# Another order for the first three memory tiles of a fused attention and expert kernel, with matmuls ahead of the first input

## The chip, the cores and the metric

The kernel runs on one core of a Trainium2 chip. A core has five engines, each with its own instruction stream: TensorE (PE, its weight loads PEld), VectorE (DVE), ScalarE (ACT), GpSimd (POOL) and SyncE (SP), which only starts transfers. The engines meet through semaphores. The metric is the device time of one execution in microseconds (us), as a median of runs.

## What is computed

One layer with a memory attention and a mixture of experts over 4 batches of 1024 tokens, 128 features each. The change touches only the attention part, cut here to what matters:

```python
z = x @ W_in                                   # 128 + 32 + query columns
z_mem = conv(pad(z[..., :160]), conv_k)        # 4 taps along the tokens
k_val = z_mem[..., :128]                       # 32 heads x 4
s_raw = z_mem[..., -32:]
log_p = clip(score_scale * s_raw, -20, 20)
p_w = exp(log_p + log_tw)                      # decayed scores; log_tw from softplus(slopes) * distance
phi = k_val[..., None] * theta                 # 8 angles each: 1024 phases per token
num_re, num_im = cumsum(p_w * cos(phi)), cumsum(p_w * sin(phi))
den = cumsum(p_w)
y = silu(read-out of (num / den) with the queries)
x = layernorm(x + y @ W_out)                   # then router, top 2 of 8 experts, shared expert, layernorm
```

## The kernel before

Four stages follow each other in each engine's stream: `memory` (the attention), `dispatch` (router, shared expert, writing the tokens to tables), `routed` (the experts) and `finish`. The change lies in `memory`.

The 4096 tokens are 32 memory tiles of 128 tokens: tile `i` is block `j = i // 4` of batch `b = i % 4`. A tile passes through these steps, which I call by the names of the helper functions:

- `phases(i)` on TensorE (L540): keys `k_val` times the angles `th_f` into the 1024 columns of PSUM tile `ph`. It waits for `frac_done` of the tile before, since `ph` exists once.
- `rounding(i)` on ScalarE (L356): the phases in turns, plus a large constant, so that they are rounded to whole turns in `feat`.
- `fraction(i)` on VectorE (L678): the phase's fraction of a turn.
- `sine(i)` (L360 absolute value, L361 Sin) and `cosine(i)` (L365) on ScalarE.
- `weigh(i)` on GpSimd (two instructions, L451): both halves of `feat` times the weights `p_tok`. It waits for `feat_done` (set by `cosine`) and for `p_kept`.
- `sums(i)` on TensorE (L556): the cumulative sum over the tile's tokens, into `nsum`.
- `read_out(i)` (two instructions, L690) and `reduce(i)` (L699) on VectorE: the sums times the queries, added up. `last_row(i, h)` on ScalarE (L374) copies the last row for the next tile of the batch; GpSimd's `carry` adds it in by a transfer.

The keys of a block of four tiles come from `value(j, t)`, four matmuls of 512 columns (L496), one per tap, into `pk`; `k_part(j)` copies them to `k_val` (L350). The weights `p_tok` are made in three chunks of 256, 256 and 512 tokens (`CHUNKS`), 32 heads x 4 batches on the partitions: `scores(n)` (L486) makes the raw scores, `keep_z(n)` copies them (L334), `logits(n)` is seven dependent instructions on VectorE (L641, three of L643, L645, L646, L649) that end in `lp_ready`, `exp_p(n)` is the exponential on ScalarE (L339), `turn_p(n)` the transposition (L507) and `keep_p(n)` the copy to `p_tok` (L344). Chunk 0 serves tiles 0 to 7, chunk 1 tiles 8 to 15, chunk 2 the rest.

What `logits` needs once is made before it on VectorE: the convolution's weights `wconv` (L622), the small operations on `sp` for the softplus of the slopes (L615 to L635, a dependent chain on one column), and the inputs of GpSimd's first instruction, which makes `th_f` (L425).

The order is written by hand: each engine has a list of calls ahead of its loop over the 32 tiles, and the loop runs ahead by `rounding(i + 3)`, `fraction(i + 3)`, `phases(i + 3)` and by `sine(i + 2)`, `cosine(i + 2)`. ScalarE's loop body of tile 0 also holds `exp_p(1)` and `exp_p(2)` with two loads of function tables around them, between `last_row(0, 1)` and `rounding(4)`. Each engine works its list in order, so a wait holds all that is behind it.

## Time and profile before

| what | value |
|---|---|
| median of 3 runs (lowest to highest) | 535.51 us (534.37 to 537.81) |
| the profiled execution's own time | 533.17 us |
| its span, first to last instruction | 531.3 us |
| busy: PE, DVE, ACT, POOL | 440.9, 376.9, 355.7, 310.1 us |
| instructions | 7487 |

The span is what the trace covers; a little under 2 us of the execution's time lie around it. The attention ends about 235 us in, dispatch about 330, the experts about 495. In the table of the 40 slices, each 13.3 us long, VectorE's digits over the attention are

```profile
DVE  7497999998999999999756566282333334554296
```

so from the fifth slice, at 53 us, to the end of the attention VectorE is busy for nine tenths or more nearly throughout, and in the four slices before that it is not.

### The profile page before, as it was taken

The page shows a single profiled execution, that of the slowest core. Times are in us where ns is not written, and L with a number is a line of the kernel's source. Part 1 is how long each engine was busy: PE and PEld are TensorE (multiplying, and loading weights), DVE is VectorE, ACT ScalarE, POOL GpSimd, SP SyncE. Part 2 cuts the span into 40 slices and gives each one's busy share as a digit, 9 for nine tenths or more (in the row PEclk, how much of TensorE's full clock was granted, in tenths as well). Part 3 has the DMA queues.
Part 4 walks back from the last instruction along what each step waited for, and adds up shares of the span by engine and source line. Part 5 has one row for each costly group of instructions (what it writes and reads, how often), then busy time and mean ns, then how long its engine had stood idle before and what let it go on. Part 6 is the DMA issues. An engine that isn't in the chain of part 4 may idle for free.

```text
span 531.3 us, 7487 instructions
## 1 busy us (share of the span) xinstructions
PE 440.9 (83%) x2153; PEld 288.9 (54%) x2153; DVE 376.9 (71%) x839; ACT 355.7 (67%) x534; POOL 310.1 (58%) x261
## 2 busy tenths in 40 slices
PE   5758899998999988856879999959999999999100
PEld 1213344433343433323657877749999999999100
DVE  7497999998999999999756566282333334554296
ACT  1848799998999999922355655617666676666244
POOL 3251567777677777761277877732555554655440
PEclk9987999999999999979689999979999999999655
DMA  7010010109866654000011111122222221221463
GB/s 258 0 40 0 2 41 1 43 15 388 313 234 226 226 209 162 1 1 1 6 48 50 47 46 51 52 70 66 67 80 68 74 63 54 68 61 46 148 227 99
DMA packets 39448, 48.55 MB, mean 91 GB/s; under 512 B 5408, under 2 KB 25058, under 8 KB 38896
## 3 DMA queue, kind: packets, MB, share of 16 engines
q1 hardware_dynamic: 34048, 39.06, 21.7%
q0 software_dynamic: 5216, 8.70, 5.3%
q10 hardware_dynamic: 144, 0.31, 0.2%
q8 instruction: 18, 0.29, 0.2%
q14 instruction: 22, 0.18, 0.1%
HBM read 19.17 MB, written 29.11 MB: 91 GB/s over the span
## 4 chain that ended last, share of the span: by engine, by line
PE 36%; DVE 33%; issue 12%; POOL 9%; ACT 7%; DMA 3%; SPq 0%; ACTq 0%; DVEq 0%; POOLq 0%
PE routed_ph L1312 12%; PE routed_po L1325 12%; DVE memory_prod L690 10%; DVE memory_y_raw L699 9%; POOL table_scratch L1017 5%; DVE memory_feat L678 4%; PE dispatch_sph L877 3%; PE dispatch_spo L887 3%; POOL memory_feat L451 2%; PE routed_px L1300 2%; DVE memory_query L673 1%; PE memory_nsum L556 1%; ACT memory_feat L356 1%; DVE finish_xo L1528 1%; ACT memory_feat L360 1%
## 5 line engine op out<-in xcount | busy, mean ns | idle before, releaser
L451 POOL TENSOR_TENSOR memory_feat<-memory_feat,memory_p_tok 128x1024 f32<-128x1024 f32 x64 | 121.6, 1923 | 57.8 <-ACT memory_feat L365 57.7
L556 PE MATMUL memory_nsum<-memory_feat,tri 128*128 128x512 f32 x256 | 118.7, 607 | 15.1 <-DVE memory_prod L690 7.3
L1288 POOL DMA_INDIRECT pick_scratch<-routed_ob,routed_xg x71 | 71.5, 1007 | 73.0 <-DVE routed_ob L1409 57.8
L556 PEld LDWEIGHTS memory_nsum<-memory_feat,tri 128*128 128x128 f32 x256 | 48.1, 194 | 76.5 <-issue 72.5
L690 DVE TENSOR_TENSOR memory_prod<-memory_nsum,memory_query 128x1024 f32<-128x1024 f32 x64 | 75.4, 1217 | 2.8 <-PE memory_nsum L556 2.7
L1017 POOL DMA_INDIRECT table_scratch<-dispatch_xrow,dispatch_slot x64 | 63.1, 986 | 18.9 <-issue 18.0
L699 DVE TENSOR_REDUCE memory_y_raw<-memory_prod 128x128 f32<-128x2048 f32 x32 | 73.1, 2285 | 1.0
L1358 ACT ACTIVATE routed_rel<-routed_ph 128x512 f32<-128x512 f32 x71 | 42.3, 597 | 45.9 <-PE routed_ph L1312 45.9
L1312 PE MATMUL routed_ph<-routed_xs,routed_w1c 128*128 128x256 f32 (+1 forms) x368 | 72.3, 340 | 0.0
L1409 DVE TENSOR_SCALAR routed_ob<-routed_po,routed_xg 128x128 f32<-128x128 f32 x71 | 22.6, 348 | 69.7 <-PE routed_po L1325 69.7
L1325 PE MATMUL routed_po<-routed_w2c,routed_hid 128*128 128x128 f32 x568 | 71.1, 275 | 0.5 <-ACT routed_hid L1367 0.5
L1325 PEld LDWEIGHTS routed_po<-routed_w2c,routed_hid 128*128 128x128 f32 x568 | 67.0, 192 | 0.8 <-ACT routed_hid L1367 0.7
L374 ACT COPY memory_last_rows<-memory_nsum 32x1024 f32<-32x1024 f32 x56 | 55.1, 1005 | 16.3 <-DVE memory_prod L690 14.0
L1312 PEld LDWEIGHTS routed_ph<-routed_xs,routed_w1c 128*128 128x128 f32 x368 | 57.3, 193 | 4.8
L540 PE MATMUL memory_ph<-setup_th_f,setup_k_val 64*128 64x512 f32 x128 | 38.0, 671 | 13.3 <-DVE memory_feat L678 12.5
L678 DVE SCALAR_TENSOR_TENSOR memory_feat<-memory_feat,memory_ph 128x1024 f32<-128x1024 f32 x32 | 38.5, 1203 | 11.5 <-ACT memory_feat L356 11.5
L1367 ACT ACTIVATE routed_hid<-routed_rel 128x512 f32<-128x512 f32 x71 | 42.5, 638 | 0.0
L496 PE MATMUL memory_pk<-memory_xT,memory_wconv 128*128 128x512 f32 x64 | 37.7, 690 | 0.4 <-issue 0.4
L887 PEld LDWEIGHTS dispatch_spo<-w,dispatch_shid 128*128 128x128 f32 x256 | 32.1, 192 | 9.8 <-issue 8.8
L365 ACT ACTIVATE memory_feat<-memory_feat,memory_half_pi 128x1024 f32<-128x1024 f32 x32 | 36.4, 1139 | 0.0
L887 PE MATMUL dispatch_spo<-w,dispatch_shid 128*128 128x128 f32 x256 | 34.3, 279 | 1.0 <-DVE y_all L1123 0.9
L877 PE MATMUL dispatch_sph<-dispatch_x1T,w 128*128 128x512 f32 x64 | 35.0, 633 | 0.0
(177 smaller groups left out, 623.8 us busy)
## 6 DMA issues: line engine op xcount, KB each, us to landing
table_scratch<-memory_blank SPq DMA_DIRECT2D x68, 260.0 KB, 2.9
finish_pick<-pick_scratch SPq DMA_DIRECT2D x16, 256.0 KB, 5.4
routed_xg<-table_scratch SPq DMA_DIRECT2D x25, 130.0 KB, 2.2
x_tok<-x SPq DMA_DIRECT2D x4, 512.0 KB, 3.8
w<-w_up SPq DMA_DIRECT2D x2, 1024.0 KB, 9.1
w<-w_down SPq DMA_DIRECT2D x2, 1024.0 KB, 11.1
out<-finish_xo SPq DMA_DIRECT2D x8, 256.0 KB, 2.3
routed_xg<-table_scratch SPq DMA_DIRECT2D x21, 65.0 KB, 1.9
```

Of the source, the lines that this page charges most:

```text
L374: nc.scalar.copy(last_rows[32 * b:32 * b + 32, h * NF:(h + 1) * NF], nsum[96:P, h * NF:(h + 1) * NF]).then_inc(rows_kept, 1)
L451: last = nc.gpsimd.tensor_tensor(v, v, pv, ALU.mult)
L556: last = nc.tensor.matmul(nsum[:, o:o + 512], tri[:], feat[:, i % U, h, q * 512:(q + 1) * 512], start=True, stop=True)
L678: nc.vector.scalar_tensor_tensor(v, v, -ROUND, ph[:], ALU.add, ALU.subtract).then_inc(frac_done, 1)
L690: nc.vector.tensor_tensor(prod[:, h, :].rearrange("p (q r c) -> p q r c", q=KQ, r=REP), nv, qv.unsqueeze(2).broadcast_to([P, KQ, REP, HM]) ...
L699: nc.vector.tensor_reduce(y_raw[:, j % 2, b, :], prod[:].rearrange("p h (c m) -> p c h m", m=M), AX.XY, ALU.add).then_inc(red_done, 1)
L877: nc.tensor.matmul(sph[q % 2][:], w1[:, E, q * P:(q + 1) * P], x1T[:, g % XR].rearrange("p t c -> p (t c)"), start=True, stop=True).then_i ...
L887: last = nc.tensor.matmul(spo[:, t * D:(t + 1) * D], shid[:, g % 2, q, t * P:(t + 1) * P], w2[:, E, q, :], start=(q == 0), stop=(q == FC - 1))
L1017: nc.gpsimd.indirect_dma_start(out=table, in_=xrow[:, r, n, :], in_offset=None, out_offset=bass.IndirectOffsetOnAxis(ap=slot[:, r, n:n + 1 ...
L1288: nc.gpsimd.indirect_dma_start(out=pick_dram, in_=ob[:, u, h, :], in_offset=None, out_offset=bass.IndirectOffsetOnAxis(ap=xg[:, t % XU, h, ...
L1312: last = nc.tensor.matmul(ph[s][:, q * n:(q + 1) * n], w1c[:, u, q * P:(q + 1) * P], xs[:, s, 0:n], start=True, stop=True)
L1325: last = nc.tensor.matmul(po[:, h * D:(h + 1) * D], hid[:, s, q * n + h * P:q * n + (h + 1) * P], w2c[:, u, q, :], start=(q == 0), stop=(q ...
```

## The change

Nothing after the loop over the tiles is changed. The lists ahead of the loops are, and some places in PSUM:

- TensorE first runs five matmuls of 256 columns on a tile of ones (`WARMING`), whose result is overwritten. VectorE sets the ones first for that.
- The keys of block 0 are made in two steps: `value_first` only those of tile 0 (four matmuls of 128 columns into `pq`), `value_rest` those of tiles 1 to 3 (four of 384 columns into `pk`). `k_first` and `k_rest` copy them. So `k_kept` and `k_done` count one more everywhere.
- `phases(0)` comes right behind `scores(0)`; `rounding(0)` comes before `exp_p(0)` on ScalarE.
- `wconv` is made before the small operations on VectorE, and so before GpSimd's `th_f`.
- VectorE's list is logits 0, fraction 0, logits 1, fraction 1, logits 2, fraction 2, query 0. It was logits 0, fraction 0, logits 1, fraction 1, fraction 2, query 0, logits 2.
- `turn_p(0)` comes behind `phases(1)`, `sums(0)` before the loop and so ahead of `phases(3)`, `k_part(1)` behind `cosine(1)`.
- The raw scores lie in `nsum` instead of `ph`.

The core of the diff:

```diff
-        z_at = (ph[:, 0:256], nsum[:, 0:256], nsum[:, 512:1024])
-        p_at = (nsum[:, 1024:1280], pq_v[:, 0:256], pq_v)
+        z_at = (nsum[:, 0:256], nsum[:, 512:768], nsum[:, 1024:1536])
+        p_at = (nsum[:, 1536:1792], pq_v[:, 0:256], pq_v)
...
+            def k_first():
+                act.wait_ge(k_done, 1)
+                nc.scalar.copy(k_val[:, 0, 0:P], pq_v[:, 0:P]).then_inc(k_kept, 1)
+
+            def k_rest():
+                act.wait_ge(k_done, 2)
+                nc.scalar.copy(k_val[:, 0, P:], pk[:, P:]).then_inc(k_kept, 1)
...
+            k_first()
             keep_z(0)
-            k_part(0)
+            rounding(0)
+            k_rest()
+            keep_z(1)
             exp_p(0)
             nc.scalar.activation(warm[:], half_pi[:], ACT.Sin).then_inc(warmed, 1)
             act.wait_ge(warmed, 1)
-            rounding(0)
+            sine(0)
+            keep_z(2)
             keep_p(0)
-            keep_z(1)
-            keep_z(2)
-            sine(0)
+            cosine(0)
             rounding(1)
-            cosine(0)
-            k_part(1)
             sine(1)
             rounding(2)
             cosine(1)
+            k_part(1)
...
+            def value_first():
+                pe.wait_ge(halo_set, 1)
+                pe.wait_ge(wconv_made, 1)
+                pe.wait_ge(x_in[0], 16)
+                for t in range(TAPS):
+                    last = nc.tensor.matmul(pq_v[:, 0:P], wconv[:, t, :], xT[:, 0, t:t + P],
+                                            start=(t == 0), stop=(t == TAPS - 1))
+                last.then_inc(k_done, 1)
+
+            def value_rest():
+                for t in range(TAPS):
+                    last = nc.tensor.matmul(pk[:, P:], wconv[:, t, :], xT[:, 1:, t:t + P],
+                                            start=(t == 0), stop=(t == TAPS - 1))
+                last.then_inc(k_done, 1)
...
+            pe.wait_ge(ones_set, 1)
+            for n in range(WARMING):
+                nc.tensor.matmul(ph[:, 0:256], one_row[:, 0:P], one_row[:, 0:256], start=True, stop=True)
             pe.wait_ge(w_arrived, 16)
+            value_first()
             scores(0)
-            pe.wait_ge(halo_set, 1)
-            pe.wait_ge(wconv_made, 1)
-            for t in range(TAPS):
-                value(0, t)
-            pe.wait_ge(z_kept, 1)
             pe.wait_ge(th_made, 1)
             phases(0)
-            pe.wait_ge(tabs_in, 32)
-            turn_p(0)
+            value_rest()
             scores(1)
             scores(2)
             phases(1)
+            pe.wait_ge(tabs_in, 32)
+            turn_p(0)
             pe.wait_ge(wq_made, 1)
             queries(0)
             for t in range(TAPS):
@@ -578,6 +605,7 @@
             phases(2)
             pe.wait_ge(p_kept, 1)
             pe.wait_ge(z_kept, 3)
+            sums(0)
             for i in range(NT):
...
+            dve.wait_ge(w_arrived, 16)
+            nc.vector.tensor_tensor(wconv[:], taps_row, w_in[:, 0:KH].unsqueeze(1).broadcast_to([P, TAPS, KH]),
+                                    ALU.mult).then_inc(wconv_made, 1)
             link(nc.vector.tensor_scalar(sp[:, 2:3], slope, -1.0, None, ALU.mult))
...
             fraction(0)
             logits(1)
             fraction(1)
+            logits(2)
             fraction(2)
             q_part(0)
-            logits(2)
```

How the instructions stand on VectorE around the third chunk of scores (`setup_lp`; 512 columns) and the tiles' `memory_feat`, before:

```order
L649 SCALAR_TENSOR_TENSOR setup_lp<-setup_dist,memory_sp,setup_lp 128x256 [waits memory_dist_in1,memory_dchain]
L678 SCALAR_TENSOR_TENSOR memory_feat<-memory_feat,memory_ph 128x1024 [waits memory_rnd_done] x2
L673 COPY memory_query<-memory_pq 128x512 [waits memory_q_done]
L641 TENSOR_SCALAR setup_lp<-setup_zs,setup_consts 128x512 [waits memory_z_kept]
L643 SCALAR_TENSOR_TENSOR setup_lp<-setup_zs,setup_consts,setup_lp 128x512 [waits memory_dchain] x3
L645 TENSOR_SCALAR setup_lp<-setup_lp,setup_consts 128x512 [waits memory_dchain]
L646 TENSOR_SCALAR setup_lp<-setup_lp 128x512 [waits memory_dchain]
```

and after the change:

```order
L678 SCALAR_TENSOR_TENSOR setup_lp<-setup_dist,memory_sp,setup_lp 128x256 [waits memory_dist_in1,memory_dchain]
L707 SCALAR_TENSOR_TENSOR memory_feat<-memory_feat,memory_ph 128x1024 [waits memory_rnd_done]
L670 TENSOR_SCALAR setup_lp<-setup_zs,setup_consts 128x512 [waits memory_z_kept]
L672 SCALAR_TENSOR_TENSOR setup_lp<-setup_zs,setup_consts,setup_lp 128x512 [waits memory_dchain] x3
L674 TENSOR_SCALAR setup_lp<-setup_lp,setup_consts 128x512 [waits memory_dchain]
L675 TENSOR_SCALAR setup_lp<-setup_lp 128x512 [waits memory_dchain]
L678 SCALAR_TENSOR_TENSOR setup_lp<-setup_dist,memory_sp,setup_lp 128x512 [waits memory_dchain]
L707 SCALAR_TENSOR_TENSOR memory_feat<-memory_feat,memory_ph 128x1024 [waits memory_rnd_done]
L702 COPY memory_query<-memory_pq 128x512 [waits memory_q_done]
```

The five rows of the third chunk now stand ahead of the third tile's remainder and of the copy of the first queries; before they stood behind both.

On ScalarE, from the exponential of the first chunk (`setup_pT`) on, before:

```order
L339 ACTIVATE setup_pT<-setup_lp 128x256 [waits memory_lp_ready]
L382 ACT_TABLE_LOAD
L382 ACTIVATE memory_warm<-memory_half_pi 128x1
L356 ACTIVATE memory_feat<-memory_ph 128x1024 [waits memory_ph_done,memory_warmed]
L344 COPY memory_p_tok<-memory_nsum 128x256 [waits memory_p_turned]
L334 COPY setup_zs<-memory_nsum 128x256 [waits memory_z_done]
L334 COPY setup_zs<-memory_nsum 128x512 [waits memory_z_done]
L360 ACTIVATE memory_feat<-memory_feat 128x1024 [waits memory_frac_done]
L361 ACTIVATE memory_feat<-memory_feat 128x1024
L356 ACTIVATE memory_feat<-memory_ph 128x1024 [waits memory_ph_done]
L365 ACTIVATE memory_feat<-memory_feat,memory_half_pi 128x1024 [waits memory_abs_done]
```

and after the change:

```order
L341 ACTIVATE setup_pT<-setup_lp 128x256 [waits memory_lp_ready]
L395 ACT_TABLE_LOAD
L395 ACTIVATE memory_warm<-memory_half_pi 128x1
L370 ACTIVATE memory_feat<-memory_feat 128x1024 [waits memory_frac_done,memory_warmed]
L371 ACTIVATE memory_feat<-memory_feat 128x1024
L336 COPY setup_zs<-memory_nsum 128x512 [waits memory_z_done]
L346 COPY memory_p_tok<-memory_nsum 128x256 [waits memory_p_turned]
L375 ACTIVATE memory_feat<-memory_feat,memory_half_pi 128x1024 [waits memory_abs_done]
L366 ACTIVATE memory_feat<-memory_ph 128x1024 [waits memory_ph_done]
L370 ACTIVATE memory_feat<-memory_feat 128x1024 [waits memory_frac_done]
```

The first rounding (L356 before) has gone from behind the table load to ahead of these rows. The second (L366 after) has gone from ahead of the first cosine (L365 before, L375 after) to behind it.

## Rows read from the trace of the kernel before

**Rows 1.** The page, part 4: the chain that ended last, by engine.

```profile
PE 36%; DVE 33%; issue 12%; POOL 9%; ACT 7%; DMA 3%; SPq 0%; ACTq 0%; DVEq 0%; POOLq 0%
```

**Rows 2.** Stretches of the span: busy time (instructions), PEclk, DMA share, GB/s.

```profile
30.00:40.00 10.00, 5.65 (x12) 2.11 (x10) 9.79 (x8) 3.95 (x4) 6.17 (x4) 0.84 0.18 53
...
60.00:100.00 40.00, 38.52 (x109) 16.41 (x109) 39.83 (x33) 38.17 (x42) 27.78 (x19) 1.00 0.11 28
```

**Rows 3.** Timeline, VectorE, to 21 us. Columns: start us, us, engine, line, operation.

```profile
4.78 2.47 DVE L622 TENSOR_TENSOR memory_wconv<-setup_consts,setup_w_in 128x512 f32<-128x512 f32 x1
...
7.18 0.14 DVE L626 TENSOR_SCALAR memory_sp<-memory_sp 128x1 f32<-128x1 f32 x1
...
13.23 0.48 DVE L649 SCALAR_TENSOR_TENSOR setup_lp<-setup_dist,memory_sp,setup_lp 128x256 f32<-128x256 f32 x1
...
17.91 0.35 DVE L641 TENSOR_SCALAR setup_lp<-setup_zs,setup_consts 128x256 f32<-128x256 f32 x1
...
20.57 0.48 DVE L649 SCALAR_TENSOR_TENSOR setup_lp<-setup_dist,memory_sp,setup_lp 128x256 f32<-128x256 f32 x1
```

**Rows 4.** Timeline, VectorE, the third scores and the first sums.

```profile
27.14 1.22 DVE L678 SCALAR_TENSOR_TENSOR memory_feat<-memory_feat,memory_ph 128x1024 f32<-128x1024 f32 x1 [4.95 <-ACT memory_feat L356]
...
28.88 1.53 DVE L641 TENSOR_SCALAR setup_lp<-setup_zs,setup_consts 128x512 f32<-128x512 f32 x1
...
30.45 3.85 DVE L643 SCALAR_TENSOR_TENSOR setup_lp<-setup_zs,setup_consts,setup_lp 128x512 f32<-128x512 f32 x3
...
34.86 2.02 DVE L646 TENSOR_SCALAR setup_lp<-setup_lp 128x512 f32<-128x512 f32 x1
...
36.91 2.28 DVE L649 SCALAR_TENSOR_TENSOR setup_lp<-setup_dist,memory_sp,setup_lp 128x512 f32<-128x512 f32 x1
...
39.11 1.21 DVE L678 SCALAR_TENSOR_TENSOR memory_feat<-memory_feat,memory_ph 128x1024 f32<-128x1024 f32 x1
...
48.45 1.22 DVE L678 SCALAR_TENSOR_TENSOR memory_feat<-memory_feat,memory_ph 128x1024 f32<-128x1024 f32 x1 [3.55 <-ACT memory_feat L356]
```

**Rows 5.** The chain in order of time: start us, us, what.

```profile
32.76 0.76 DVE setup_lp L643
```

**Rows 6.** Timeline, GpSimd, to 39 us.

```profile
4.75 1.95 POOL L425 TENSOR_TENSOR setup_th_f<-setup_consts,setup_theta 128x1024 f32<-128x1024 f32 x1 [4.31 <-DVE setup_theta L617]
...
22.05 3.78 POOL L451 TENSOR_TENSOR memory_feat<-memory_feat,memory_p_tok 128x1024 f32<-128x1024 f32 x2 [12.01 <-ACT memory_feat L365]
...
28.22 3.96 POOL L451 TENSOR_TENSOR memory_feat<-memory_feat,memory_p_tok 128x1024 f32<-128x1024 f32 x2 [2.38 <-ACT memory_feat L365]
...
34.65 3.99 POOL L451 TENSOR_TENSOR memory_feat<-memory_feat,memory_p_tok 128x1024 f32<-128x1024 f32 x2 [2.47 <-ACT memory_feat L365]
```

**Rows 7.** Timeline, ScalarE, to 44 us.

```profile
13.75 0.42 ACT L339 ACTIVATE setup_pT<-setup_lp 128x256 f32<-128x256 f32 x1 [0.18 <-DVE setup_lp L649]
...
15.48 0.20 ACT L382 ACTIVATE memory_warm<-memory_half_pi 128x1 f32<-128x1 f32 x1
...
16.89 0.88 ACT L334 COPY setup_zs<-memory_nsum 128x256 f32<-128x256 f32 x2
...
18.03 1.06 ACT L360 ACTIVATE memory_feat<-memory_feat 128x1024 f32<-128x1024 f32 x1 [0.26 <-DVE memory_feat L678]
...
33.44 1.14 ACT L365 ACTIVATE memory_feat<-memory_feat,memory_half_pi 128x1024 f32<-128x1024 f32 x1
...
41.48 2.14 ACT L374 COPY memory_last_rows<-memory_nsum 32x1024 f32<-32x1024 f32 x2 [6.91 <-DVE memory_prod L690]
```

**Rows 8.** Timeline, TensorE, to 31 us.

```profile
5.84 1.08 PE L486 MATMUL memory_ph<-memory_xT,setup_w_in 128*32 128x256 f32 x8 [5.84 <-DMA memory_xT<-x_T]
...
13.71 1.13 PE L540 MATMUL memory_ph<-setup_th_f,setup_k_val 64*128 64x512 f32 x4 [0.77 <-ACT setup_k_val L350]
...
20.07 3.60 PE L496 MATMUL memory_pk<-memory_xT,memory_wconv 128*128 128x512 f32 x8
...
28.51 2.08 PE L540 MATMUL memory_ph<-setup_th_f,setup_k_val 64*128 64x512 f32 x4 [3.78 <-DVE memory_feat L678]
```

More of the change, by code:

```diff
@@ L51 @@
 EPS = 1e-5
+WARMING = 5
 MemoryStage = namedtuple("MemoryStage", "sync fill scalar gpsimd tensor vector y_done frac_done k_kept q_kept "
@@ L249, in memory @@
         halo_set = sem("halo_set")
+        ones_set = sem("ones_set")
         dchain = sem("dchain")
@@ L344, in keep_p @@
                 nc.scalar.copy(p_tok[:, a // P:e // P].rearrange("p j b k -> p (j b k)"), p_at[n]).then_inc(p_kept, 1)
+            def k_first():
[4 more added lines that the diff above has]
+                nc.scalar.copy(k_val[:, 0, P:], pk[:, P:]).then_inc(k_kept, 1)
             def k_part(j):
-                act.wait_ge(k_done, j + 1)
+                act.wait_ge(k_done, j + 2)
                 if j >= 2:
@@ L405, in scalar @@
                     keep_p(i // 2 - 1)
-                if j + 1 < TPB:
+                if i < NT - B:
                     last_row(i, 0)
@@ L493, in value @@
                     pe.wait_ge(x_in[0 if j < 2 else 1 if j < 4 else 2], 16)
-                    if j:
-                        pe.wait_ge(k_kept, j)
+                    pe.wait_ge(k_kept, j + 1)
                 ins = nc.tensor.matmul(pk[:], wconv[:, t, :], xT[:, :, j * P + t:j * P + t + P],
@@ L533, in phases @@
                 j, b = i // B, i % B
-                if b == 0:
-                    pe.wait_ge(k_kept, j + 1)
+                if i == 0:
+                    pe.wait_ge(k_kept, 1)
+                elif i == 1 or b == 0:
+                    pe.wait_ge(k_kept, j + 2)
                 if i:
@@ L588, in tensor @@
                     queries((i + 1) // 2)
-                sums(i)
+                if i:
+                    sums(i)
                 if i in (4, 6):
@@ L603, in link @@
                 dve.wait_ge(dchain, n[0])
+            nc.vector.memset(one_row[:], 1.0).then_inc(ones_set, 1)
             nc.vector.memset(half_pi[:], HALF_PI)
             nc.vector.memset(xT[:, :, 0:HALO], 0.0)
-            nc.vector.memset(one_row[:], 1.0)
             nc.vector.memset(blank[:], 0.0).then_inc(dchain, 1)
@@ L620, in vector @@
             nc.vector.tensor_scalar(ncoef[:], coef[:], -1.0, None, ALU.mult).then_inc(coef_done, 1)
-            dve.wait_ge(w_arrived, 16)
-            nc.vector.tensor_tensor(wconv[:], taps_row, w_in[:, 0:KH].unsqueeze(1).broadcast_to([P, TAPS, KH]),
-                                    ALU.mult).then_inc(wconv_made, 1)
             dve.wait_ge(soft_exp, 1)
@@ L835, in turn_x @@
                 else:
-                    pe.wait_ge(mem.k_kept, TPB)
+                    pe.wait_ge(mem.k_kept, TPB + 1)
                 for t in range(GT):
```

## The prediction

> **What bounds the kernel now.** I began with the page: its chain is TensorE for 36% and VectorE for 33% of the span [rows 1], so no engine bounds the whole. The stretches separate them: from 60 to 100 us VectorE is busy for 39.83 of 40 us and ScalarE for 38.17 [rows 2]. The attention is thus bound by VectorE once its loop runs, and what comes ahead of the loop costs in full what it delays the loop. From there I read the timeline engine by engine. The reader is to see three losses on VectorE. It waits 4.95 us for the third rounding, until 27.14 [rows 4]. The third chunk's scores take from 28.88 to 39.11, 10.2 us, though one of their steps takes 0.76 us where nothing disturbs it [rows 4, 5]. And it waits 3.55 us at 48.45 for ScalarE, which loads two tables behind the first tile's last rows [rows 4, 7].
>
> The 10.2 us are a collision. GpSimd's `weigh` is on from 28.22 to 32.18 and from 34.65 to 38.64 [rows 6]; L641 and the first L643, then L646 (2.02 us) and L649 (2.28 us), end each just after one of its four instructions of about 1.9 us [rows 4, 6]. The two engines take turns, instruction by instruction. The same is seen at 4.78: `wconv` takes 2.47 us and ends 0.55 after `th_f`, which ran from 4.75 to 6.70 [rows 3, 6].
>
> **The start, to 13.7 us.** `wconv` now goes first and needs those 0.55 us alone, so `th_f` starts some 0.7 later, at about 5.5, and ends at 7.45. The softplus chain began at 7.18 and led to the first scores, which ended at 13.71 [rows 3]. It could begin at 5.7 now, but its third operation reads two operands from SBUF, like `wconv`, and I let it wait for `th_f`: then it stands at 7.5, where it stood before, and the first scores still end at 13.7. If it does not wait, 1.5 us are gained (a rival below); a loss is at most 0.2.
>
> The Trainium skill, page "SBUF — State Buffer", section "SBUF: two separate sides", says that VectorE and GpSimd share a port pair as an exclusive lock held for a whole instruction, and that VectorE needs it for two SBUF inputs or a two-port mode. By that rule the third operation does wait, the sum keeps its 13.7, and scores that overlap `weigh` are held wherever they are put; the 2.02 us of L646 agree.
>
> The warm-up matmuls: four matmuls of 512 columns take 3.60 us [rows 8], so one of 256 takes 0.45 at that rate and 0.9 at half. Five take 2.3 to 4.5 us from about 1.4 on, and end by 5.9, when the input comes (TensorE's first matmul waits for it until 5.84 [rows 8]). They cost nothing. Even at half rate (2.08 us for a tile's phases, against 1.13 [rows 8]) the first phases are there by 10 and rounded by 11, and VectorE can use them at 13.7: 2.7 us hide all that TensorE does in this part, the split of the keys and its extra instructions too.
>
> **13.7 to 21.8 us: a gain given back.** The first remainder starts at 13.7 instead of 16.8 (ScalarE waits for its end until 18.03 before [rows 7]); it ends at 14.95, and the second scores, 3.14 us long (17.91 to 21.05 [rows 3]), end at 18.1. But the second remainder needs `rounding(1)`, which now stands behind `cosine(0)`. ScalarE's exponential starts at 13.75 as before, and table and first Sin end at 15.68 [rows 7]. Then come absolute value and Sin at 0.95 each, copies of 512 and 256 columns at 0.88 together [rows 7], the cosine at 1.14 (that of the third tile [rows 7]), done at 19.65, and the rounding at about 1.0: 20.6. It was ready for the remainder at 21.05 before. Of 3 us only 0.45 are left; VectorE idles for 2.5 instead, and `fraction(1)` ends at 21.8.
>
> **21.8 us on: the third scores.** Undisturbed they would take 4.7 us: the 3.14 of 256 columns, plus 0.28 for each of four two-input operations (0.48 to 0.76 [rows 3, 5]) and about half as much for each of the other three. But GpSimd starts earlier as well: `cosine(0)` ends at 19.65 and `weigh(0)`, 3.78 us long [rows 6], is on until 23.5. The first operation waits 1.7. `weigh(1)` comes when `cosine(1)` ends: 21.8 + 1.9 + 0.95 + 1.14 = 25.9. TensorE is not late for that, since the second keys (3.60 us) fill its time from 17.8 to 21.4. By 26.2 VectorE has done four of seven; the fifth and sixth then wait for one instruction of GpSimd each, 1.85 and 1.65. Sum: 21.8 + 4.7 + 1.7 + 3.5 = 31.7, or 31.2 if the overlaps at the instructions' ends count as in the 10.2 us before; I take 31.5. The bounds are 26.5 (no wait at all) and 34.1 (four waits of 1.9). So the scores stand ahead of the third remainder, but not ahead of GpSimd's work.
>
> **To the loop.** `fraction(2)` starts at 31.5. Before, from its start at 27.14 to the end of `cosine(2)` at 34.58 it was 7.44 us [rows 4, 7], with the 2.08 us of phases at half rate after TensorE had waited 3.78 [rows 8]. It has waited at least that now: `sums(0)`, moved ahead of `phases(3)`, is over by 23.5 + 3.7 = 27.2, hence blocks nothing. So `cosine(2)` ends at 38.95. VectorE's remainder and first half of the read-out are done by 38.5 and wait for nobody, so the last rows start at 39.0; before they started at 41.48, waiting for VectorE [rows 7]. From there to the remainder at 48.45 it was 6.97 us [rows 4, 7], with 0.14 of waiting for the second half, which goes: 6.85. That remainder now starts at 45.85, **2.6 us earlier**. Between bounds it is 0.0 (34.1) to 7.6 (26.5). `k_part(1)`, moved behind the cosine, is needed only by the fifth tile.
>
> Behind that point the four lists are the same, all hang on ScalarE's fourth tile, and the transfers of tokens, weights and table blanks are released by `ph_done`, so they move along. VectorE has 0.17 us of slack in 40, which is no room for the gain to be lost in. I carry the 2.6 to the end: 533.2 becomes 530.6 for the profiled execution, which lay 2.3 under the median; the median becomes 535.5 - 2.6 = **532.9**.
>
> **Rivals.**
> - *The chain does not wait for `th_f`.* Small operations went on beside GpSimd for long, but those have one input. The first scores end 1.5 us earlier; ScalarE's copies of rest keys and scores (until 12.4) leave 1.3 of it: 531.6. Chance 0.12.
> - *The third scores escape.* If `weigh(1)` comes 1.3 us later than 25.9 or the scores start as much earlier, one wait or both fall away; with both the scores end at 28.2 and 3.3 us more are gained: 529.6, and with no wait at all 527.9. For it: a late `phases(2)` would do it, for instance TensorE at half rate. Against: ScalarE's sum is made of measured durations. Chance 0.17.
> - *Nothing is gained.* The collisions take their upper bound, or a wait of GpSimd or ScalarE that I don't see takes the 2.6 us back: 535.5. For it: the scores' 9.7 us are nearly the 10.2 of before. Chance 0.18.
> - *Slower.* TensorE's 36% [rows 1] lie mostly in the expert stage. If the shift makes the granted clock fall there for longer, work takes 1.84 times as long (2.08 to 1.13). From 9.5 us of such work on, it is slower by over 1%; with 10, 532.9 + 8.4 = 541.3. Against: nothing of that stage is changed. Chance 0.03.
>
> **How the numbers follow.** The forecast has 0.50, with a range of its own of 531.6 to 534.3 (scores' end from 30 to 33). A measurement of this kernel can tell about 1%, 5.4 us, from no change. Only the escape passes that on the fast side, so faster has 0.17, slower 0.03, within 1% 0.80. From 529.2 to 535.8 the range holds all but the far part of the escape and the slow case.
>
> **What would show it.** In the changed kernel's timeline: the first remainder at about 13.7; VectorE idle for about 2.5 us before the second, released by ScalarE's rounding; `weigh(0)` at 19.7; L670 to L678 at 512 columns from 21.8 to 31.5, three of them prolonged to over 1.5 us; the first last rows at 39; the remainder after the table loads at 45.9. I am wrong if the 512-column scores take under 7 us, if the remainder at 45.9 is outside 44.5 to 47.2, or if the loop's shift is not found again at the end of the attention, at about 235.

## The result and the profile after

Over 8 runs beside 8 runs of the kernel before, the changed kernel took **531.72 us** (530.05 to 533.28), the kernel before 535.58 (534.37 to 537.81). The ratio is **0.9922 [0.9899, 0.9945]**: 3.9 us faster, with an interval of 2.9 to 5.4. The same kernel again, later and beside 10 other runs of before (`c1_changed_again`), gave 0.9923 [0.9895, 0.9951]. The forecast was 532.9, within 1% of before; both hold. In what follows a ratio leaves out the slow runs, those over 1.5% above the fastest of their kernel (three of before, two of e6); a median doesn't.

| | before | after |
|---|---|---|
| median | 535.58 | 531.72 |
| profiled execution, its span | 533.2, 531.3 | 531.0, 529.2 |
| busy PE, DVE, ACT, POOL | 440.9, 376.9, 355.7, 310.1 | 444.5, 375.8, 356.0, 310.5 |
| VectorE reaches dispatch at | 228.88 | 225.35 |

The timeline of VectorE, after (start us, us, engine, line, operation, and in brackets the idle time before it and what ended it):

```profile
5.98 1.55 DVE L657 TENSOR_TENSOR memory_sp<-memory_sp 128x1 f32<-128x1 f32 x1
...
13.31 0.48 DVE L678 SCALAR_TENSOR_TENSOR setup_lp<-setup_dist,memory_sp,setup_lp 128x256 f32<-128x256 f32 x1
13.71 1.22 DVE L707 SCALAR_TENSOR_TENSOR memory_feat<-memory_feat,memory_ph 128x1024 f32<-128x1024 f32 x1
...
20.54 1.22 DVE L707 SCALAR_TENSOR_TENSOR memory_feat<-memory_feat,memory_ph 128x1024 f32<-128x1024 f32 x1 [2.54 <-ACT memory_feat L366]
21.68 2.06 DVE L670 TENSOR_SCALAR setup_lp<-setup_zs,setup_consts 128x512 f32<-128x512 f32 x1
...
26.13 2.02 DVE L674 TENSOR_SCALAR setup_lp<-setup_lp,setup_consts 128x512 f32<-128x512 f32 x1
28.18 2.02 DVE L675 TENSOR_SCALAR setup_lp<-setup_lp 128x512 f32<-128x512 f32 x1
...
30.90 1.21 DVE L707 SCALAR_TENSOR_TENSOR memory_feat<-memory_feat,memory_ph 128x1024 f32<-128x1024 f32 x1
...
35.34 1.22 DVE L707 SCALAR_TENSOR_TENSOR memory_feat<-memory_feat,memory_ph 128x1024 f32<-128x1024 f32 x1 [2.63 <-ACT memory_feat L366]
...
45.01 1.22 DVE L707 SCALAR_TENSOR_TENSOR memory_feat<-memory_feat,memory_ph 128x1024 f32<-128x1024 f32 x1 [3.86 <-ACT memory_feat L366]
```

Where the first two remainders stood in before (there L678):

```profile
16.77 1.22 DVE L678 SCALAR_TENSOR_TENSOR memory_feat<-memory_feat,memory_ph 128x1024 f32<-128x1024 f32 x1 [3.05 <-ACT memory_feat L356]
...
20.98 1.22 DVE L678 SCALAR_TENSOR_TENSOR memory_feat<-memory_feat,memory_ph 128x1024 f32<-128x1024 f32 x1
```

So the first remainder starts at 13.71 instead of 16.77, but the second at 20.54 instead of 20.98, behind 2.54 us of idle time that ScalarE's rounding ends. The third scores (L670 to L678, 512 columns) run from 21.68 to 30.98, 9.3 us against 10.3 [rows 4] (10.2 if counted to the start of the next step). The fifth remainder, my landmark ahead of the loop, starts at 45.01 instead of 48.45.

GpSimd, after:

```profile
5.57 1.95 POOL L436 TENSOR_TENSOR setup_th_f<-setup_consts,setup_theta 128x1024 f32<-128x1024 f32 x1 [5.13 <-DVE setup_theta L649]
...
19.67 3.78 POOL L462 TENSOR_TENSOR memory_feat<-memory_feat,memory_p_tok 128x1024 f32<-128x1024 f32 x2 [8.82 <-ACT memory_feat L375]
25.82 4.09 POOL L462 TENSOR_TENSOR memory_feat<-memory_feat,memory_p_tok 128x1024 f32<-128x1024 f32 x2 [2.37 <-ACT memory_feat L375]
```

`weigh(0)` comes at 19.67 and `weigh(1)` at 25.82, 2.4 us earlier than in [rows 6], so each still lies in the third scores. ScalarE, after:

```profile
11.79 0.48 ACT L354 COPY setup_k_val<-memory_pk 128x384 f32<-128x384 f32 x1 [1.75 <-PE memory_pk L522]
...
13.83 0.42 ACT L341 ACTIVATE setup_pT<-setup_lp 128x256 f32<-128x256 f32 x1 [1.07 <-DVE setup_lp L678]
...
19.48 1.02 ACT L366 ACTIVATE memory_feat<-memory_ph 128x1024 f32<-128x1024 f32 x1
...
34.29 1.02 ACT L366 ACTIVATE memory_feat<-memory_ph 128x1024 f32<-128x1024 f32 x1 [8.07 <-PE memory_ph L567]
...
38.26 1.92 ACT L384 COPY memory_last_rows<-memory_nsum 32x1024 f32<-32x1024 f32 x2
```

TensorE, after:

```profile
1.45 4.63 PE L589 MATMUL memory_ph<-setup_one_row 128*128 128x256 f32 x10 [1.45 <-DVE setup_one_row L634]
...
7.84 1.13 PE L567 MATMUL memory_ph<-setup_th_f,setup_k_val 64*128 64x512 f32 x4
...
32.16 2.08 PE L567 MATMUL memory_ph<-setup_th_f,setup_k_val 64*128 64x512 f32 x4 [4.90 <-DVE memory_feat L707]
```

The warm-ups (ten records for five matmuls) end at 6.1, and the first tile's phases then take 1.13 us. The page's chain has VectorE at 30%, 3 points less than in [rows 1]. The gain of the landmark is still there where VectorE leaves the attention, in the first instruction of dispatch, before and after:

```profile
228.88 0.06 DVE L1044 MEMSET dispatch_minus_half<- 128x4 f32 x1
```

```profile
225.35 0.06 DVE L1073 MEMSET dispatch_minus_half<- 128x4 f32 x1
```

That is 3.53 us. The two spans differ by 2.1 only, because the first 16 expert matmuls went faster in before's profiled execution than in after's: 4.43 us from 357.54 on against 5.68 us from 353.92. In all the thirteen other than before's they took 5.09 to 6.69 us, so before's 4.43 is the exception, and I don't put these 1.25 us down to the change. The shift in front of them, 3.62 us, is near the 3.9 of the medians.

### The profile page after: what moved, and what is told of

Same layout as the page of the kernel before. It is cut to its first block, busy times and chain, and to the rows that moved or that the text cites. A ratio compares the mean times of both kernels' runs of the same rounds, so it can differ in the third digit from the quotient of the medians.

```text
span 529.2 us, 7525 instructions
## 1 busy us (share of the span) xinstructions
PE 444.5 (84%) x2171; PEld 293.3 (55%) x2171; DVE 375.8 (71%) x839; ACT 356.0 (67%) x535; POOL 310.5 (59%) x261
## 4 chain that ended last, share of the span: by engine, by line
PE 38%; DVE 30%; issue 11%; POOL 9%; ACT 8%; DMA 3%; SPq 0%; ACTq 0%; DVEq 0%; POOLq 0%
PE routed_ph L1341 13%; PE routed_po L1354 12%; DVE memory_prod L719 8%; DVE memory_y_raw L728 8%; POOL table_scratch L1046 5%; DVE memory_feat L707 4%; PE dispatch_spo L916 3%; PE memory_nsum L583 3%; PE dispatch_sph L906 3%; POOL memory_feat L462 2%; PE routed_px L1329 2%; ACT memory_feat L366 1%; ACT memory_feat L370 1%; DVE finish_xo L1557 1%; ACT memory_feat L375 1%
## 5 line engine op out<-in xcount | busy, mean ns | idle before, releaser
L1341 PE MATMUL routed_ph<-routed_xs,routed_w1c 128*128 128x256 f32 (+1 forms) x368 | 73.5, 344 | 0.0
L366 ACT ACTIVATE memory_feat<-memory_ph 128x1024 f32<-128x1024 f32 x32 | 32.8, 1024 | 9.4 <-PE memory_ph L567 8.7
L375 ACT ACTIVATE memory_feat<-memory_feat,memory_half_pi 128x1024 f32<-128x1024 f32 x32 | 36.5, 1139 | 0.0
L370 ACT ACTIVATE memory_feat<-memory_feat 128x1024 f32<-128x1024 f32 x32 | 33.7, 1053 | 1.3 <-DVE memory_feat L707 1.3
## 6 DMA issues: line engine op xcount, KB each, us to landing
w<-w_down SPq DMA_DIRECT2D x2, 1024.0 KB, 11.3
```

What stands on the lines that cost most here:

```text
L1341: last = nc.tensor.matmul(ph[s][:, q * n:(q + 1) * n], w1c[:, u, q * P:(q + 1) * P], xs[:, s, 0:n], start=True, stop=True)
```

## The experiments

My theory: the start of the loop is late by GpSimd's `weigh(1)`, which takes turns with the third scores although nobody needs its result yet, and by ScalarE's exponentials behind the last rows; the order line alone buys little. Rivals: the order line is what gave the 3.4 us at the landmark; or the warm-ups and the split of the keys did; or the wait for ScalarE's rounding ahead of the second remainder is what costs.

All runs in one table. Times count from the start of the last step of the first scores (13.31 in after), since the inputs' arrival moves everything by up to 0.4 us. "Scores" is the length of the third scores. "Dispatch" is VectorE's first instruction of that stage. Each ratio is taken against runs of before on the same chip: their median was 536.17 beside e1 to e4, 555.33 beside e5 to e8, 536.13 beside c1 and e9 to e11. "One" marks a single run.

| run | time, us | ratio | 2nd remainder | scores | landmark | dispatch |
|---|---|---|---|---|---|---|
| before | 535.58 | | 7.75 | 10.3 | 35.22 | 215.65 |
| after | 531.72 | 0.9922 [0.9899, 0.9945] | 7.23 | 9.3 | 31.70 | 212.04 |
| c1 | 531.58 | 0.9923 [0.9895, 0.9951] | 7.22 | 9.3 | 31.70 | 212.65 |
| e1 | 533.70 | 0.9944 [0.9922, 0.9966] | 7.22 | 10.4 | 32.86 | 214.93 |
| e2 | 536.49 | 1.0012 [0.9991, 1.0033] | 7.74 | 10.9 | 35.65 | 216.14 |
| e3 | 526.95 | 0.9816 [0.9781, 0.9851] | 7.22 | 6.2 | 27.64 | 209.80 |
| e4 | 529.39 | 0.9862 [0.9826, 0.9898] | 7.22 | 9.3 | 27.96 | 209.99 |
| e5 | 547.33 | 0.9871 [0.9821, 0.9921] | 7.23 | 6.2 | 23.89 | 204.31 |
| e6 | 553.80 | 0.9957 [0.9913, 1.0001] | 8.37 | 9.3 | 31.91 | 212.39 |
| e7 | 554.58, one | | 5.43 | 10.8 | 30.45 | 212.41 |
| e8 | 553.96, one | | 7.22 | 9.3 | 31.70 | 212.18 |
| e9 | 534.88, one | | 7.74 | 10.3 | 33.91 | 215.77 |
| e10 | 533.73, one | | 10.00 | 7.8 | 32.71 | 214.57 |
| e11 | 524.82 | 0.9782 [0.9759, 0.9805] | 7.22 | 6.2 | 23.88 | 204.94 |

e5 to e8 ran on a chip on which the kernel before took some 20 us more too; the attention was as fast there as elsewhere, and the 20 us lie behind it (last section).

### The order line, taken back and alone

`e1_scores_back` is the changed kernel with

```diff
             fraction(1)
-            logits(2)
             fraction(2)
             q_part(0)
+            logits(2)
```

> The changed kernel, with only the third chunk's scores put back behind the third remainder and the copy of the first queries on VectorE. Landmark: the start of the fifth remainder (the one behind ScalarE's two table loads), 48.45 us before and 45.01 after. Theory A (collisions with GpSimd decide, wherever the scores stand): the third remainder runs at 24.7, the scores from 26.5 to some 33.5 to 35, the phases of the fourth tile come earlier, and the landmark lies at about 44.4, from 43 to 45.5: the undone line was worth nothing or cost a little, time 531.7 less 0.6. Rival B (the gain comes from having the scores ahead of the third remainder): most of the 3.4 us go back, landmark 47.5 or later, time about 534.5.

VectorE's timeline of this run:

```profile
26.22 1.54 DVE L670 TENSOR_SCALAR setup_lp<-setup_zs,setup_consts 128x512 f32<-128x512 f32 x1
...
45.92 1.22 DVE L707 SCALAR_TENSOR_TENSOR memory_feat<-memory_feat,memory_ph 128x1024 f32<-128x1024 f32 x1 [3.55 <-ACT memory_feat L366]
```

The landmark comes 1.16 us later than in the same kernel with the line, counted as in the table. The scores ran from 26.22 to 36.65, held as in [rows 4]. So of the 3.5 us, some 1.2 hang on the line. That lies between the two ranges that I had given: the line is worth more than my theory said and less than the rival did.

`e2_scores_only` is the kernel before with this line alone, the other way round.

> The kernel before, with only the third chunk's scores put ahead of the third remainder on VectorE. Theory A: the scores start at 22.2, meet both pairs of GpSimd's instructions (22.05 to 25.8 and 28.2 to 32.1) and end at 32.8; the third remainder follows, and the fifth, the landmark (48.45 before), starts at 47.1, 1.4 us earlier; time 534.2. Rival B (this line is what gains): the landmark comes at 45 to 45.5 and the time is about 532.

```profile
33.19 1.21 DVE L678 SCALAR_TENSOR_TENSOR memory_feat<-memory_feat,memory_ph 128x1024 f32<-128x1024 f32 x1
...
40.39 1.23 DVE L690 TENSOR_TENSOR memory_prod<-memory_nsum,memory_query 128x1024 f32<-128x1024 f32 x1 [1.45 <-PE memory_nsum L556]
```

The scores ended 6.2 us earlier than before, but the third remainder (L678 at 33.19) started 5.8 later, and the first read-out (L690) waited 1.45 us for TensorE's sums, which in this list stand behind the phases and keys of the fourth tile. The landmark is 0.4 us later and the ratio 1.0012. My expectation had left the place of `sums(0)` out. I conclude that the line needs the move of `sums(0)` ahead of the loop; no run has these two alone.

### GpSimd's second turn held back

`e3_hold_weigh` keeps `weigh(1)` off until the third scores are done. Nothing is left out, and the sums of that tile are needed late enough:

```diff
                 pool.wait_ge(p_kept, 1 if j < 2 else 2 if j < 4 else 3)
+                if i == 1:
+                    pool.wait_ge(lp_ready, 3)
```

> The changed kernel, with one wait more: GpSimd's second weighting waits until the third chunk's scores are done. Theory A: only the first of the seven scores' operations is still held; they end at 27.5 instead of 30.98, the fourth tile's phases follow TensorE's idle time of only 1.4 us and run at full rate, and the landmark lies at 40.9 to 41.8 instead of 45.01; time about 528.1. Rival C (the collisions cost VectorE nothing that the end feels, or GpSimd's delay of 1.7 us is itself on the path): landmark at 45 or later, time 531.7 or more.

```profile
25.77 0.49 DVE L676 TENSOR_SCALAR setup_lp<-setup_lp,setup_consts 128x512 f32<-128x512 f32 x1
26.29 0.43 DVE L677 TENSOR_SCALAR setup_lp<-setup_lp 128x512 f32<-128x512 f32 x1
...
27.42 1.21 DVE L709 SCALAR_TENSOR_TENSOR memory_feat<-memory_feat,memory_ph 128x1024 f32<-128x1024 f32 x1
...
40.59 1.22 DVE L709 SCALAR_TENSOR_TENSOR memory_feat<-memory_feat,memory_ph 128x1024 f32<-128x1024 f32 x1 [3.86 <-ACT memory_feat L366]
```

```profile
27.67 3.78 POOL L464 TENSOR_TENSOR memory_feat<-memory_feat,memory_p_tok 128x1024 f32<-128x1024 f32 x2 [4.59 <-DVE setup_lp L680]
```

The two steps that took 2.02 us each in after take 0.49 and 0.43 (L676, L677). The scores are 3.1 us shorter, and `weigh(1)` starts at 27.67 behind them, about 2.2 us late, without anyone waiting for it. A further 0.94 came from TensorE, as expected: it was idle 1.78 us instead of 4.90 ahead of the fourth tile's phases, and they took 1.13 us instead of 2.08. (The granted clock was 1.00 of 2.4 GHz from 28 to 36.5 us here, and 0.50, so 1.2 GHz, from 32 to 40 in after.) Sum 4.06, the landmark's gain over after. This shows that 3.1 of the scores' 9.3 us were the collision with `weigh(1)`; the first hold, beside `weigh(0)`, is still there (L672 follows at 23.41, as in after). The ratio is 0.9816, its interval clear of after's.

### The exponentials taken out of the loop

`e4_exp_early` moves ScalarE's exponentials of chunks 1 and 2, with their table loads, ahead of the loop:

```diff
             k_part(1)
+            exp_p(1)
+            exp_p(2)
+            nc.scalar.activation(warm[:], half_pi[:], ACT.Silu)
             for i in range(NT):
...
-                if i == 0:
-                    exp_p(1)
-                    exp_p(2)
-                    nc.scalar.activation(warm[:], half_pi[:], ACT.Silu)
```

> The changed kernel, with the exponentials of chunks 1 and 2 and the two table loads around them moved on ScalarE from behind the first tile's last rows to ahead of the fourth rounding, where ScalarE idled for 8.07 us after the change. Theory A: they run from 31.05 to 34.8, make the fourth rounding 0.5 us late, and the 3.86 us that VectorE waited at the landmark go: it lies at 41.7 instead of 45.01; time about 528.4. Rival D (VectorE is not what bounds the attention at that point, so the waiting only moves): the landmark comes earlier, but the end of the attention moves by less than 1.5 us and the time is 530.5 or more.

```profile
30.70 0.63 ACT L341 ACTIVATE setup_pT<-setup_lp 128x512 f32<-128x512 f32 x1 [3.07 <-DVE setup_lp L677]
...
33.98 1.02 ACT L366 ACTIVATE memory_feat<-memory_ph 128x1024 f32<-128x1024 f32 x1 [1.13 <-PE memory_ph L566]
...
39.90 1.02 ACT L366 ACTIVATE memory_feat<-memory_ph 128x1024 f32<-128x1024 f32 x1
```

ScalarE waited 8.07 us in after (L366 at 34.29) while VectorE worked on the scores. The exponential of chunk 1 fits in there, that of chunk 2 starts at 30.70, as soon as the scores are done, and the table load is over while TensorE still makes the phases. The rounding of the fifth tile then comes right behind the last rows, VectorE has no idle time ahead of the landmark, and the landmark is 3.74 us earlier. The expectation, 41.7, stood 0.4 later if counted as in the table: chunk 1 need not wait for the third scores, which I had not used.

### Both

`e5_hold_exp` has both edits; `e11_both_again` is the same kernel on another chip.

> Both edits of the two last experiments on the changed kernel: GpSimd's second weighting waits for the third chunk's scores, and the exponentials of chunks 1 and 2 stand with their table loads ahead of the fourth rounding. The scores end at 27.5, the exponentials and loads then run to about 30.6 behind them, as the first load no longer has to wait; the fourth rounding follows at about 30.7 instead of 29.9. The landmark (the fifth remainder, 45.01 after, 40.59 and 40.96 with one edit each) should lie at 37.3 to 38.2. Theory A, that VectorE bounds everything behind it: the time falls by the same 7 us against the changed kernel, to about 525. Rival D (another engine becomes the bound when the loop starts so early, for instance GpSimd, whose second weighting now ends at 31.5): the landmark comes at 39 or later, or the shift is lost by 100 us.

> The kernel with both edits (GpSimd's second weighting held, exponentials early) once more, beside the changed kernel. On the chip of its first run every kernel was some 20 us slower behind the attention. Theory A: landmark 36.9 again, 11.6 us ahead of the kernel before and 8.1 ahead of the changed one; the attention's shift was kept to its end (VectorE's first setup operation of the dispatch at 217.3 against 225.4), so the time should be 535.6 - 11.5 = 524, ratio 0.979, and 8 us under the changed kernel. Rival: a part of it is given back behind the attention, as the first run's ratio of 0.987 suggests; then the ratio lies at 0.985 or above and some stage behind 240 us starts less than 11 us ahead.

```profile
36.78 1.22 DVE L708 SCALAR_TENSOR_TENSOR memory_feat<-memory_feat,memory_ph 128x1024 f32<-128x1024 f32 x1
```

The landmark is 7.82 us earlier than in after, against 4.06 + 3.74 = 7.80 for the two apart: they add. The median is **524.82 us** (523.24 to 525.28), ratio 0.9782 [0.9759, 0.9805]: 11.3 us under before and 6.8 under the changed kernel beside it, where I had expected 11.5 and 8. On the other chip the ratio was 0.9871, with the landmark in the same place and dispatch 0.6 us earlier. This version beats both kernels.

### The parts at the start

`e6_no_warm` leaves out the five matmuls on the tile of ones (`WARMING = 0`, no wait for the ones).

> The changed kernel without the five matmuls ahead of the input. Prediction as on record: 2.7 us of cover hide TensorE's part at half rate, so nothing changes: landmark 45.0. Read again with the changed kernel's trace I expect less cover: the rest of the first keys (2.85 us at full rate, twice that at half) stands ahead of the second scores' copy and of the first exponential on ScalarE, which waited only 1.07 us for VectorE; with half rate until 9 to 11 us the exponential comes 0 to 1.2 us late, and the landmark lies between 45.0 and 46.2; time at most 1.2 us more. A rival on which the warm-up is what gains: landmark 47 or later.

```profile
5.95 2.04 PE L516 MATMUL memory_pq<-memory_xT,memory_wconv 128*128 128x128 f32 x8 [5.95 <-DMA memory_xT<-x_T]
...
33.10 1.13 PE L567 MATMUL memory_ph<-setup_th_f,setup_k_val 64*128 64x512 f32 x4 [3.21 <-DVE memory_feat L704]
```

```profile
13.89 0.48 ACT L354 COPY setup_k_val<-memory_pk 128x384 f32<-128x384 f32 x1 [1.80 <-PE memory_pk L522]
...
14.76 0.42 ACT L341 ACTIVATE setup_pT<-setup_lp 128x256 f32<-128x256 f32 x1
```

The first keys took 2.04 us instead of 1.47 and the first phases 2.08 instead of 1.13. ScalarE's copy of the other keys (L354) came at 13.89 instead of 11.79, the exponential at 14.76 instead of 13.83, and the second remainder 1.14 us later. Then 0.93 came back: TensorE had been idle 3.21 us, not 4.90, ahead of the fourth tile's phases, and they took 1.13 us and not 2.08. At the landmark 0.2 are left. The ratio of 0.9957 [0.9913, 1.0001] adds nothing to that, as the changed kernel didn't run on this chip.

`e7_round_first` puts the second rounding ahead of the first cosine:

```diff
             sine(0)
+            rounding(1)
             keep_z(2)
             keep_p(0)
             cosine(0)
-            rounding(1)
```

> The changed kernel, with the second rounding put directly behind the first tile's first Sin on ScalarE, ahead of two copies and the cosine. VectorE's wait of 2.54 us ahead of the second remainder shrinks to 0.7, and the third scores start at 19.9 instead of 21.7. Theory A (turns with GpSimd): the first weighting starts at 20.6, one us later, and now meets three of the seven operations instead of one, the second again two; the scores end at 30.5 to 31, as before (30.98), and the landmark lies within 0.5 us of 45.0: the 1.8 us are lost in the collision. Rival E (the wait of 2.54 us was the loss, as it reads in the profile): landmark at 43.2.

```profile
18.46 1.22 DVE L707 SCALAR_TENSOR_TENSOR memory_feat<-memory_feat,memory_ph 128x1024 f32<-128x1024 f32 x1 [0.75 <-ACT memory_feat L366]
...
20.12 5.39 DVE L672 SCALAR_TENSOR_TENSOR setup_lp<-setup_zs,setup_consts,setup_lp 128x512 f32<-128x512 f32 x3
```

```profile
25.11 6.47 PE L583 MATMUL memory_nsum<-memory_feat,tri 128*128 128x512 f32 x8 [3.45 <-POOL memory_feat L462]
31.58 1.13 PE L567 MATMUL memory_ph<-setup_th_f,setup_k_val 64*128 64x512 f32 x4
```

The second remainder comes 1.8 us earlier, as meant. The scores then start at 19.60 and meet GpSimd four times instead of three; `L672` alone takes 5.39 us for three steps, and of the 1.8 us 0.3 are left at their end. The landmark is 1.25 us earlier, outside the 0.5 of my expectation: the other 0.9 came from TensorE, whose `sums(0)`, started later and slower, ran until 31.58, so that it went straight on to the phases, at 1.13 us. The wait for the rounding was thus hardly what cost: an earlier start of the scores is eaten by GpSimd.

`e8_keys_whole` makes and copies the keys of block 0 in one piece again, behind the first raw scores, with the semaphores' counts kept (the list on TensorE; ScalarE's follows it):

```diff
-            value_first()
             scores(0)
+            value_first()
...
-            value_rest()
```

> The changed kernel, with the first tile's keys no longer made alone: the scores first, then the keys of all four tiles in four matmuls of 512 columns and one copy, then the first phases, as in the kernel before. TensorE ends the keys at 10.7, the first phases at 12.4 and ScalarE the first rounding at 13.5, just ahead of the first remainder at 13.7; the second scores are copied by 13.9. Theory A: landmark 45.0 to 45.3, so the split is worth nothing by itself. Rival: it is what gained the 3 us at the first remainder; landmark 46.5 or later.

The landmark stands at 31.70 in both. The split of the keys gives nothing.

`e9_k_part_only` is the kernel before with ScalarE's `k_part(1)` moved from behind `cosine(0)` to behind `cosine(1)`, and nothing else.

> The kernel before, with only the copy of the second keys (k_part(1)) moved on ScalarE from ahead of the second tile's sine to behind its cosine. Before, that copy waited until 23.71 for TensorE and held the sine, which could start at 22.2. Expected: the third rounding at 24.7 instead of 26.1, the third remainder at 25.8 instead of 27.1, the third scores end at 37.7 instead of 39.2, landmark 47.0 instead of 48.45. A rival, that ScalarE has room there: landmark 48.2 to 48.5.

```profile
25.62 1.22 DVE L678 SCALAR_TENSOR_TENSOR memory_feat<-memory_feat,memory_ph 128x1024 f32<-128x1024 f32 x1 [3.64 <-ACT memory_feat L356]
```

The landmark is 1.31 us earlier than in before: the copy had stood ahead of the third rounding, for which VectorE waited 4.95 us [rows 4]. It waits 3.64 now.

`e10_round_late` is the changed kernel with `rounding(0)` put back behind the table load.

> The changed kernel, with only the first rounding put back behind the first exponential and its table load on ScalarE, where it stood before. The first remainder starts at 16.8 instead of 13.7, the second rounding ends at 23 instead of 20.5, the third scores end at 33.4 instead of 31.0. By durations alone the landmark lies at 47.4; TensorE idles less ahead of the fourth phases (sums(0) ends later), so that these may run at full rate and give 1 us back: 46.4. Rival, by which the early first rounding is worth nothing since its gain was given back at the second remainder (2.54 us of waiting there): landmark 45.5 or earlier.

```profile
29.26 0.43 DVE L675 TENSOR_SCALAR setup_lp<-setup_lp 128x512 f32<-128x512 f32 x1
29.72 2.33 DVE L678 SCALAR_TENSOR_TENSOR setup_lp<-setup_dist,memory_sp,setup_lp 128x512 f32<-128x512 f32 x1
```

```profile
18.05 2.08 PE L567 MATMUL memory_ph<-setup_th_f,setup_k_val 64*128 64x512 f32 x4 [4.79 <-DVE memory_feat L707]
...
22.24 4.11 PE L506 MATMUL memory_pk<-memory_xT,memory_wconv 128*128 128x512 f32 x8
26.28 1.13 PE L567 MATMUL memory_ph<-setup_th_f,setup_k_val 64*128 64x512 f32 x4
```

The first remainder starts at 16.68, 3.1 us later counted as above, but the landmark only 1.0 later. The late start spared the scores. TensorE, idle for 4.79 us, made the second phases at half its rate (2.08 us) and the keys behind them in 4.11, not 3.60. So the third phases came at 26.28 only; their rounding stands ahead of `cosine(1)`, and `weigh(1)` started at 29.60. L674 and L675 (0.49 and 0.43) were not held, only L678 was (2.33 instead of 0.75), so that one hold of three fell away and the scores took 7.8 us. It is the smaller half of the escape that the prediction had as a rival, brought about by the very mechanism it named, TensorE at half rate.

The changed kernel itself, beside e9, e10 and e11:

> The changed kernel as it is, once more, on the chip of the three runs beside it. Its ratio to the kernel before should be 0.992 again (0.990 to 0.995), its landmark (start of the fifth remainder) 45.0. The other kernels of this group are to be read against it.

Its landmark stands at 31.70 again; at dispatch it is 0.6 us later than in after.

### Where a gain at the landmark is lost again

The last two columns of the table don't move together. The distance from the landmark to dispatch is 180.3 to 180.5 us in before, after, e2, e5, e6 and e8, 181.0 and 181.1 in c1 and e11, and 181.9 to 182.2 in e1, e3, e4, e7, e9 and e10. Read-out by read-out the kernels run in step up to tile 12, and the difference of the last six arises there, at about 120 us, in one place: TensorE waits some 2 us for the second half of GpSimd's `weigh`, and the eight matmuls of the sums behind that wait take 3.67 us or up to 5.37. (In c1 and e11 they took 3.67; there 0.6 us go at the sums behind, which waited 0.80 and 0.92 us for GpSimd.) TensorE's timeline in after, e6, e3 and e10:

```profile
124.23 3.67 PE L583 MATMUL memory_nsum<-memory_feat,tri 128*128 128x512 f32 x8 [2.20 <-POOL memory_feat L462]
```

```profile
124.51 3.67 PE L583 MATMUL memory_nsum<-memory_feat,tri 128*128 128x512 f32 x8 [2.47 <-POOL memory_feat L462]
```

```profile
120.08 5.37 PE L585 MATMUL memory_nsum<-memory_feat,tri 128*128 128x512 f32 x8 [2.47 <-POOL memory_feat L464]
```

```profile
125.06 5.37 PE L583 MATMUL memory_nsum<-memory_feat,tri 128*128 128x512 f32 x8 [2.19 <-POOL memory_feat L462]
```

Idle times of 2.20 and 2.47 us led to the one, 2.47 and 2.19 to the other. So the length of the wait doesn't decide it. The granted clock goes with it: from 118 to 130 us its mean is 0.86 in e1, e3, e4, e7, e9 and e10 and 1.00 in the other eight, and in e3 it is 0.50, the lower of TensorE's two levels (1.2 GHz), from 122 to 124 us. What makes it fall in one execution and not in the next, I can't say; the rows show that it did in 6 of 14 profiled executions, that this costs 1.5 to 1.8 us in each, and no link with what was changed ahead of it. That e3's profiled execution was the longest of its four (529.3; the others 526.1 to 527.6) fits a thing that differs between executions of one kernel. No run here tests it. It may also be why a single time of e9 (534.88), which has the loss in its trace, shows nothing of the 1.3 us that it gained at the landmark.

## Why the prediction was right

Step by step, with what each measured:

- **First scores at 13.7**: 13.79, first remainder 13.71. L657, the third operation of the softplus chain, took 1.55 us beside `th_f` (5.57 to 7.52) where its neighbours took 0.16. The chain did wait, and that rival fell at once. The Trainium skill's page "SBUF — State Buffer", section "SBUF: two separate sides", says that an instruction of VectorE with two SBUF inputs waits for the whole of an instruction of GpSimd that reads SBUF and started first. The trace agrees, even for one column: `th_f` ran from 5.57 to 7.52, L657 from 5.98 to 7.53.
- **Warm-ups cost nothing**: right, they end at 6.1 and the input's matmuls start at 5.88. **"2.7 us hide all that TensorE does in this part"**: wrong. I had measured the cover on VectorE, from the rounding to the remainder. The tighter one is on ScalarE, where the copies of the other keys and raw scores now stand ahead of the exponential; its slack is 1.07 us (L341 in after), and e6 went past it. Of the 1.14 us that this cost at the second remainder, 0.2 reached the landmark, since the phases later gave the rest back. That so little was left is the doing of those phases, not of the cover.
- **A gain given back at the second remainder**: idle 2.5 forecast, 2.54 measured; start 20.6, measured 20.54.
- **The third scores**: `weigh(0)` 19.7 and 19.67, `weigh(1)` 25.9 and 25.82; the first, fifth and sixth steps held, as forecast. (The terms given for `weigh(1)` add to 25.8, not 25.9, and those for `cosine(0)` to 19.6; neither slip matters.) The term was a little mis-sized: undisturbed the seven steps take 4.6 us (9.3 less the three holds, as e3 shows with 0.49 and 0.43), but a hold is 1.6 us and not 1.65 to 1.85. Three make 4.7 and not 5.2, and the end came at 30.98 instead of 31.5.
- **To the landmark**: last rows at 38.26 instead of 39.0, of which 0.6 are the scores; from there 6.75 instead of 6.85. Landmark 45.01 instead of 45.85: 3.44 us of gain where 2.6 stood in the sum.
- **Carried to the end**: 3.53 at dispatch, 3.62 at the experts, 3.9 in the medians. Of the 1.2 us between forecast and median, 0.8 are those of the landmark; the median lies just inside the main case's range, 531.6 to 534.3. But that the shift is carried was luck in part: "behind that point the four lists are the same" left out that TensorE's rate differs between executions. In six other profiles 1.5 to 1.8 us were lost at tile 12; before and after are both without that loss.
- **The rivals**: the escape was not this kernel's but came by one step in e10 and, on purpose, by two in e3. There the two steps gave 3.1 us where I had 3.3, and with the 0.94 of the phases at full rate, which I had left out, 4.06 at the landmark. "Nothing is gained" and "slower" did not come.

Where the 3.5 us came from can only be told in parts that don't add: 1.2 hang on the line with the third scores (e1), 1.0 on the early first rounding (e10), 1.3 on `k_part(1)` where it was tried alone (e9), about 0.2 on the warm-ups (e6), none on the split of the keys (e8). The move of `sums(0)` wasn't tried alone; e2 shows only that in the lists of before, where it isn't made, the line costs 0.4.

## What to carry to other kernels

When a chain of small steps on one engine takes turns with another engine's long instructions, moving the chain earlier moves the collision with it; hold back the other engine's work, if nobody needs it yet, with one wait. Ahead of the loop, follow each gain to the next wait: 3 us won at the first tile were about 0.5 one tile later. And put table loads and exponentials into the longest idle time of their engine rather than behind the work that everybody waits for.

## What the hardware showed that I had not expected

- A step of 0.43 us took 2.02 us when it had to wait for its turn beside GpSimd, and three that take 2.33 together took 5.39 (e7). A two-input operation on a single column was held for 1.55 us.
- TensorE's rate after a wait of some 2 to 3 us can't be told from the wait's length. The same four phase matmuls took 1.13 us after 1.78 or 3.21 us of idle time, 1.86 after 2.20 and 2.08 after 2.47, 4.79 or 4.90; eight sums took 3.67 or 5.37 after the same 2.47. Steps late by 1 us were so made up by phases at the full rate (e6), and gains of 1.5 us lost (e3, e4).
- The granted clock doesn't show every slow matmul. From 6 to 11 us it is 1.00 in after and in e6 alike, and yet the first phases took 1.13 us in the one and 2.08 in the other.
- Two chips ran the attention alike, and what follows it took 326.0 us on the one (e5) and 303.6 on the other (e11), with the same kernel. The stretch from 270 to 350 us of e5 and of e11, one kernel on two chips (busy time and instructions of PE, PEld, DVE, ACT and POOL, then the granted clock, the DMA share and GB/s):

```profile
270.00:350.00 80.00, 68.13 (x393) 52.72 (x393) 37.49 (x225) 37.46 (x69) 48.66 (x50) 0.89 0.12 38
```

```profile
270.00:350.00 80.00, 72.98 (x466) 57.79 (x465) 46.83 (x248) 41.67 (x77) 55.05 (x56) 0.96 0.18 55
```

The granted clock is 0.89 in the one and 0.96 in the other, and TensorE issued 393 matmuls against 466 in the same time.
